# A one-block transformer layer on eight cores: two activation buffers swapped, bf16 weight copies spread over two blocks, and the weight's affine step moved to the middle of a tile

## The reference, cut to what matters

```
x: (8, 2048, 4096)
h   = layernorm(x) @ Wqkv            # 32 query heads of 128, ONE shared key head and value head
a   = softmax(causal(q k^T * 128**-0.5 + alibi slope * (pos_k - pos_q))) v
x1  = x + layernorm(a @ Wo)
h   = relu(s0 * (layernorm(x1) @ (2*k0 - 1))) * 2      # k0, k1, k2 are boolean matrices, 4096 x 4096
h   = relu(s1 * (ei(h) @ (2*k1 - 1))) * 2              # ei: features from 3277 on times -4
out = x1 + layernorm(s2 * (ei(h) @ (2*k2 - 1)))
```

## Time and profile before

| what | value |
|---|---|
| three runs | 5302.34, 5311.39, 5714.11 us |
| profiled execution | 5305.34 us, its span 5303.7 us (core 5, the slowest) |
| spans of the cores | 5267.9 to 5303.7 us |
| mean granted clock of TensorE | 0.988 to 0.992 |
| TensorE matmul busy | 5100.2 us, 96% |
| VectorE, ScalarE busy | 1697.2 us, 1404.5 us |

### The profile page before, as it was taken

How to read it: one execution, slowest core, us unless ns; L and a number is a source line. 1 busy time by engine, 2 the same in 40 slices (tenths; PEclk the granted TensorE clock), 3 DMA queues, 4 the chain that set the end, 5 groups by cost and what they waited for, 6 DMA issues and landing times.

```text
span 5303.7 us, 74679 instructions; the slowest of 8 cores (5267.9 to 5303.7 us)
## 1 busy us (share of the span) xinstructions
PE 5100.2 (96%) x28386; PEld 2512.8 (47%) x28386; DVE 1697.2 (32%) x3061; ACT 1404.5 (26%) x3331; POOL 467.1 (9%) x750
## 2 busy tenths in 40 slices
PE   6999989999989999999999999999999999999998
PEld 4544444455434444455554444455555444444443
DVE  3332212344323331233432333123333114343235
ACT  3321112333100111554430011166555101100002
POOL 0000001111110000000000000000000000101111
PEclk9999999999999999999999999999999999999999
DMA  8779999989999756332234666633222346465487
GB/s 178 135 135 194 185 203 200 212 197 195 203 220 252 243 207 223 134 120 104 104 119 152 221 231 222 213 129 105 96 88 96 136 151 235 174 257 191 151 302 292
DMA packets 125056, 955.24 MB, mean 180 GB/s; under 512 B 14819, under 2 KB 14948, under 8 KB 15076
## 3 DMA queue, kind: packets, MB, share of 16 engines
q0 software_dynamic: 101088, 782.29, 53.9%
q1 hardware_dynamic: 23620, 168.18, 8.8%
HBM read 839.26 MB, written 136.31 MB: 184 GB/s over the span
## 4 chain that ended last, share of the span: by engine, by line
PE 85%; DMA 10%; DVE 2%; issue 1%; DVEq 1%; ACT 1%; SPq 0%; ACTq 0%; POOLq 0%
PE pb L584 47%; PE pb L621 28%; PE pb L492 5%; PE pb L521 4%; DMA wst<-k 4%; DMA wst<-wq 2%; DMA xf<-x1sp 2%; DMA out<-xf 1%; PE pb L535 1%; DVEq L800 1%; DMA Vx<-x 1%; PE pb L506 1%; DMA xf<-x 0%; PE pb L572 0%; DVE xf L770 0%
## 5 line engine op out<-in xcount | busy, mean ns | idle before, releaser
L983 ACT ACTIVATE PT<-pb,eb_sb 128x64 bf16<-128x64 f32 (+4 forms) x2720 | 1012.6, 438 | 1035.6 <-PE pb L521 512.1
L584 PE MATMUL pb<-Ub,wst 128*128 128x512 bf16 x4096 | 1004.6, 379 | 0.0
L584 PE MATMUL pb<-Xb,wst 128*128 128x512 bf16 x4192 | 935.4, 379 | 28.6 <-DMA wst<-wq 22.3
L621 PE MATMUL pb<-wst,Vx 128*128 128x512 bf16 x4096 | 898.5, 382 | 30.3 <-DVE wst L684 28.0
L621 PE MATMUL pb<-wst,Qb 128*128 128x512 bf16 x4096 | 901.8, 382 | 7.9 <-DMA wst<-wob 5.8
L684 DVE TENSOR_SCALAR wst<-wst 128x4096 bf16<-128x4096 bf16 x416 | 518.7, 1248 | 878.6 <-DMA wst<-k 878.5
L584 PE MATMUL pb<-Vx,wst 128*128 128x512 bf16 x3072 | 746.6, 380 | 1.3 <-DVE Qb L807 1.3
L621 PEld LDWEIGHTS pb<-wst,Vx 128*128 128x128 bf16 x4096 | 401.5, 98 | 519.8 <-issue 49.7
L584 PEld LDWEIGHTS pb<-Xb,wst 128*128 128x128 bf16 x4192 | 404.2, 98 | 492.5 <-issue 36.4
L621 PEld LDWEIGHTS pb<-wst,Qb 128*128 128x128 bf16 x4096 | 400.8, 98 | 486.2 <-issue 19.9
L584 PEld LDWEIGHTS pb<-Ub,wst 128*128 128x128 bf16 x4096 | 395.7, 98 | 374.9 <-issue 2.2
(11 more groups left out here) (74 smaller groups left out, 1830.3 us busy)
## 6 DMA issues: line engine op xcount, KB each, us to landing
wst<-k POOLq DMA_DIRECT2D x416, 1024.0 KB, 5.4
wst<-wob POOLq DMA_DIRECT2D x96, 1024.0 KB, 5.2
wst<-wq POOLq DMA_DIRECT2D x68, 1024.0 KB, 13.6
wst<-wqb POOLq DMA_DIRECT2D x68, 1024.0 KB, 6.3
xf<-x SPq DMA_DIRECT2D x56, 1024.0 KB, 10.5
wqb<-wq POOLq DMA_DIRECT2D x34, 1024.0 KB, 19.4
wst<-wo POOLq DMA_DIRECT2D x32, 1024.0 KB, 13.0
x1sp<-xf SPq DMA_DIRECT2D x32, 1024.0 KB, 7.2
```

What stands on the lines that cost most here:

```text
L584: m = t.matmul(pb[b][:, :], w[:, c * 128:(c + 1) * 128], fm(src, c), start=(c == 0), stop=(c == 31))
L621: m = t.matmul(pb[b][:, :], src[:, c * TB + tl * 128: c * TB + tl * 128 + 128], w[:, ii * 512:(ii + 1) * 512], start=(c == 0), stop=(c == 31))
L983: m = s.activation(PT[:, g % 4, off:off + w], pb[S0 + g % 2][:, off:off + w], AF.Exp, bias=eb[:, col:col + 1], scale=SCALE)
```

## The change

Four things are edited; no arithmetic changes.

1. The buffers are swapped: `ln0` (and so `qkv`) uses `Vx`, `ln1` (and so `f1`) uses `Xb`. Beside `wo(1)` and `wo(2)`, `ln0` now goes ahead of `ln2`, in VectorE's steps and in the load order, with its transposes at tiles 5, 9, 13 and 17. What is left of the steps beside a `wo` stage is done by VectorE in the next `qkv` stage, after the stage's statistics and before `ln1`. The transposes of `ln1` beside `qkv(2)` and `qkv(3)` are at 9, 15, 21, 27 and not at 6, 12, 18, 24, and ScalarE computes the residual's scale after the evacuation of tile 3, not of tile 0.
2. The 66 copies are spread over the k tiles of block 0 and block 1 (one behind about one in three); the 32 of Wo are all issued by the 93rd of the 96 k tiles of block 0. Before `wo(1)` the queue waits for these 32 alone, and for the 34 of Wqkv before `qkv(3)`.
3. `qkv(2)` therefore reads Wqkv in f32.
4. In `f1` and `f2` VectorE does the affine step at position 9 of the 16, not ahead of position 0. `f3` is left as it is.

```diff
 for _st in ORDER:
+    for _k, _i in LN_AT.get(_st, []):
+        XUSE += [(_k, _i, tl) for tl in range(4)]
     if _st in LN2_AT:
         XUSE += [(2, LN2_AT[_st], tl) for tl in range(4)]
-    for _k, _i in LN_AT.get(_st, []):
-        XUSE += [(_k, _i, tl) for tl in range(4)]
...
     if stage in LN2_AT:
-        return [15 + 5 * tl for tl in range(4)], [13 + 5 * tl for tl in range(4)]
+        return [5 + 4 * tl for tl in range(4)], [3 + 4 * tl for tl in range(4)]
+    if stage[0] == "qkv" and stage[1] > 1:
+        return [9 + 6 * tl for tl in range(4)], [7 + 6 * tl for tl in range(4)]
     return [6 + 6 * tl for tl in range(4)], [4 + 6 * tl for tl in range(4)]
...
-    LN_DST = {0: Xb, 1: Vx}
+    LN_DST = {0: Vx, 1: Xb}
...
                     if stage == ("wo", 1):
-                        gp.wait_ge(sCvt, 16 * 66)
+                        gp.wait_ge(sCvt, 16 * 32)
+                    if stage == ("qkv", 3):
+                        gp.wait_ge(sCvq, 16 * 34)
...
-                            src = (wq_h if i < 2 else wqb_h)[QKV_ORDER[p]]
+                            src = (wq_h if i < 3 else wqb_h)[QKV_ORDER[p]]
...
-                        if kind in LAYER and i == 0:
+                        if kind in LAYER and i < 2:
                             nf += 1
-                            if ncvt < nf * 66 // 96:
+                            if ncvt < nf * 66 // 190:
...
-                            for _ in ln1(i - 1):
-                                pass
+                            for side in rest + [ln1(i - 1)]:
+                                for _ in side:
+                                    pass
...
                         for p in range(32):
-                            affine_to(AFFB[stage] + min(p + 3, ahead))
                             for e in range(16):
+                                if e == 9:
+                                    affine_to(AFFB[stage] + min(p + 3, ahead))
...
-                        sides = []
+                        sides = [ln0(li) if k == 0 else ln1(li)
+                                 for k, li in LN_AT.get(stage, [])]
                         if stage in LN2_AT:
                             sides.append(ln2(LN2_AT[stage]))
-                        for k, li in LN_AT.get(stage, []):
-                            sides.append(ln0(li) if k == 0 else ln1(li))
...
-                        for side in sides:
-                            for _ in side:
-                                pass
+                        if kind == "wo":
+                            rest = sides
+                        else:
+                            for side in sides:
+                                for _ in side:
+                                    pass
                         slice_stats(stage, 7, src, st)
...
-                            if p == 0 and i > 0:
+                            if i > 0 and p == (3 if i > 1 else 0):
                                 rstd(("y", i - 1), mvy[:, :, 1], rsy[:, :])
```

More of the change, by code:

```diff
@@ L304, in build_program @@
     sCvt = sem("sCvt")
+    sCvq = sem("sCvq")
     sAff = sem("sAff")
@@ L393, in _ @@
                                                  in_=wq_h[ncvt - 32]
-                                                 ).then_inc(sCvt, 16)
+                                                 ).then_inc(sCvq, 16)
                                 ncvt += 1
@@ L403, in _ @@
                     for hf in range(2):
-                        sy.dma_start(out=rows32(Ub, Vx, tl)[:, hf * 2048:(hf + 1) * 2048],
+                        sy.dma_start(out=rows32(Ub, Xb, tl)[:, hf * 2048:(hf + 1) * 2048],
                                      in_=x_h[tl * 128:(tl + 1) * 128,
@@ L552, in first_kv @@
                         for c in range(32):
-                            xs = Xb[:, c * TB + tl * 128:c * TB + tl * 128 + 128]
+                            xs = Vx[:, c * TB + tl * 128:c * TB + tl * 128 + 128]
                             wc = w[:, c * 128:(c + 1) * 128]
@@ L649, in _ @@
                         tw.wait_ge(sTev, 16 * (LNI[0, i] + 1))
-                        feature_major(stage, Xb, att_due(0) if i == 0 else NO_ATT, 0, 0, 33)
+                        feature_major(stage, Vx, att_due(0) if i == 0 else NO_ATT, 0, 0, 33)
                         if i == 0:
@@ L691, in row_stats @@
                     L = 4 * LNI[kind, i] + tl
-                    rows = rows32(Ub, Vx, tl) if L < 4 else xf
+                    rows = rows32(Ub, Xb, tl) if L < 4 else xf
                     for j in range(8):
@@ L705, in normalise @@
                     if L < 4:
-                        rows, dst = rows32(Ub, Vx, tl), tm(Qb, tl, 0, D)
+                        rows, dst = rows32(Ub, Xb, tl), tm(Qb, tl, 0, D)
                     else:
```

## The result

The changed kernel takes 0.9873 of the time of the kernel before, 95% interval 0.983 to 0.9915. The profiled execution of before took 5305.3 us. Of the profiled execution of after I read core 5: its span is 5230.8 us, against 5303.7 for core 5 of before.

A forecast was written before the change was run, and what follows sets the result against it. TensorE was taken as the bound, computing 5100.2 of 5303.7 us. Terms -27 - 16 + 3 + 2 + 23 - 14 - 14 - 4 - 1 = -48 us took 5305.3 to 5257, stated as 5258; range 5232 to 5298 for 8 in 10.

The forecast's parts named there:

- The sign and the bound: Whole kernel: without taking away TensorE work, the change wins back at most its idle 203.5 us, 3.8%.
- rival C: In stage qkv(2), the fetch has enough lead: +3 and not +23 us, total 5238; 8%.
- Copies, block 0, `f3(0)`: Fewer copies bring f3(0) down to its sister stage f3(1), less 3 us left for meetings: -27 us.
- Copies, block 0, `f1(0)` and `f2(0)`: Of 18.8 us of TensorE waits for attention there, 3 stay: -16 us, bounds 0 and -18.8.
- Affine step at position 9: Beside attention, the step no longer runs back to back with the evacuation: -4 us in block 2, -1 in block 1.
- Copies, block 1: The 34 transfers moved here are hidden by the fetch's lead: f3(1) +3 us, f1(1) and f2(1) +2.
- Rival B: A copy costs TensorE the same in block 0 or 1, so moving 34 gains nothing: about 5298 us; 15%.
- `qkv(2)`: Reading f32 weights in this stage makes it longer: +23 us, between 3 and 45.
- a clock that falls from 1.00: Sign that the forecast is wrong: a stage's clock falls that was at 1.00; no size given.
- Buffer swap: In wo(1) and wo(2), ln0 going first removes TensorE's wait for zn: -14 us each.
- Rival D: In the wo stages the wait for zn stays, at tile 9, 13 or 17, about 12 us each: 5286 us; 12%.
- Rival E: Mid-tile affine step holds up mask or normalisation in VectorE's order, 0.71 us in each of 192 tiles: 5375 us; 5%.

The follow-up runs named there:

- copies alone: Kernel before with the copies spread over blocks 0 and 1, two separate waits and f32 weights in stage qkv(2); span 5292.3 us, ratio 0.9964.

## Why the prediction was right or wrong

**The sign and the bound.** Right: the gain lies within TensorE's idle time before. The 5239 us are within 5232 to 5298, near its low end; the forecast of 5258 lay 19 us above. That the range held is partly luck: its low end was set for rival C, which did not occur, and terms that missed by 39 us of gain were set off by others that missed by 14 us of loss (below).

**Copies, block 0, `f3(0)`.** Right: -29.9 for -27. The sister stage was the measure, and the 3 us left for meetings of a k tile with a copy did not occur. The DMA share was forecast at 81% in `f3` and came at 0.74 and 0.67, and at 63% and 59% beside the two attentions, where 0.63 and 0.51 came: the 7.3 us of a copy, taken from the full stage, are too much where the engines are less full.

**Copies, block 0, `f1(0)` and `f2(0)`.** This is the step that failed: "-16 (bounds 0 and -18.8)", where -29.0 came, outside the bounds. The mechanism, stalls behind VectorE's waits for k tiles, was right; the size was not. I bounded the gain by the listed waits of the earlier trace rows. The idle time alone was 20.35 us, and 8.6 us more were matmuls that took longer, most of it at the lower granted clock, which show as busy time. On the other cores of before the gain is 13.6 to 26.8 us, on four of the seven over the bound too. For `wo(1)`, `f3(0)` and `qkv(1)` I had set a stage beside its sister, which holds both; here, having none of the same length, I fell back on waits alone.

**Affine step at position 9.** The mechanism was right, evacuation and affine step back to back, and the size was off: -10.3 for -4 beside block 3's attention, -6.8 for -1 beside block 2's. The affine step put back showed -6.2 to be the step's alone in block 2. For block 3, I took a third of the 13.5 us of the earlier trace rows by weighing new meetings against old; 3.6 us of waits are left after, and position 3 did no worse than 9, so there are few new meetings. For block 2 I had -1 of 4.7 us idle; 4.3 of these went, and TensorE was busy for 600.9 us before and 598.3 after. That difference of 2.5 us is not the granted clock, which was 1.00 in both, and stays open. It was also wrong to give the step no share of its own in block 1: alone it wins 24 us there, with the copies left where they were.

**Copies, block 1.** +2 and +3 for nothing. The reason given, the three tiles' lead of the fetch and shares far from 1, fits the kernels that carried 34 copies there with the affine step in either place; neither the lead nor the share was varied by itself. Rival B, 15%, is out by `f3(1)`, 223.3 us with and without copies.

**`qkv(2)`.** +23 for +26.3, and 26.3 comes from f32 alone. On the cores at 0.99 of the six kernels with the stage in f32 it lasted 262.9 to 269.3 us, 21 to 27 more than in bf16, so the 3 us are within scatter, and whether the full buffers handed over by `wo(1)` bought anything can't be told. Rival C is out. One of the prediction's signs of being wrong did appear, a clock that falls from 1.00: it is 0.98 here, and of the 26.3 us 19.0 are idle and 7.3 longer busy time. The Trainium skill's page "SBUF — State Buffer" (section on the bandwidth-pool intuition that is wrong) gives about 358 GB/s between memory and a core, by which the stage would have been 3 us longer; it was 26.3. By the same count of bytes the stage moved 88 MB in 268.5 us, 328 GB/s, an estimate 8% under the page's figure, and the DMA engines' share was 1.01 at that: near the figure, but too far under it to price the stage by.

**Buffer swap.** -16.2 and -16.1 for -14 and -14; alone -14.4 and -14.5. Rival D, 12%, did not occur. On VectorE's timeline of after, the second row of `ln0` in `wo(1)` is normalised from 1655.71 to 1658.12, and its first transposes, in tile 9, run at 1676.15: 18 us to spare where I had estimated 7. VectorE's wait there is for ScalarE's scale, no longer for a load.

```profile
1655.71 2.41 DVE L714 TENSOR_SCALAR zn<-xf,mvx,rsx 128x4096 bf16<-128x4096 f32 x1 [17.12 <-ACT rsx L951]
```

**Rival E.** Not seen: no attention stage became longer. Its price of 0.71 us for every meeting was the worst of its parts: of the four places tried, 3 and 9 are within 1 us of each other, and only the two at the tile's boundary cost 3 us or more over them.

**The end.** +6.5 us was no term of the sum at all, and 4.9 of them are GpSimd's closing DRAIN, 8.55 for 3.65 us.

**By terms**, the sum of -48 missed -72.9 by 25 us: 27 from the three attention stretches, 10 from `f3(0)`, `f3(1)` and the `wo` stages, 2 from block 3, against 3 from `qkv(2)`, 5 from the start and `qkv(1)`, and 6.5 from the end.

## What to carry to other kernels

Size a stall by a sister stage, or by the stretch's whole time against its matmuls, not by the listed waits: here matmuls at three of them ran at half clock and counted as busy. Look at all the cores before taking one stage's stall for the program's. Try the long instruction of a side engine that works in order a few positions away from another one at the boundary; here that was worth nearly as much as taking away the wait in front of it. Background transfers cost nothing at a DMA share of 0.83 here and much at 1, so filling stages to about that level beat spreading evenly.

## What the runs showed of the hardware

That casting copies behind about one k tile in three did not cost TensorE 0.1 us in `f3(1)`, at a DMA share of 0.67 (after) to 0.72 (copies alone), was better than I had expected.

```profile
2707.87:2931.14 223.27, 221.18 (x1026) 100.13 (x1024) 55.33 (x61) 18.97 (x32) 29.55 (x43) 1.00 0.67 198
```

```profile
2735.51:2958.77 223.26, 221.18 (x1026) 100.13 (x1024) 55.33 (x61) 18.93 (x32) 24.53 (x43) 1.00 0.72 198
```

What I had not expected at all was the time behind the last instruction, 5 us longer in all kernels that issue copies in block 1, with nothing busy on any engine and no byte moving while GpSimd's DRAIN runs.

```profile
5222.00:5223.00 1.00, 0.00 (x0) 0.00 (x0) 0.00 (x0) 0.00 (x0) 0.00 (x0) 0.50 0.00 0
...
5230.00:5231.00 1.00, 0.00 (x0) 0.00 (x0) 0.00 (x0) 0.00 (x0) 0.00 (x0) 0.50 0.00 0
```

These are single microseconds of after behind the last store: in both the DMA share is 0.00 and every engine is idle, while the span runs on to 5230.8.
